# Earlier gate weights, smaller first LayerNorm groups, and a moved token mean in a macaron of routed experts, attention and a mixer

## The chip, the core and the metric

The kernel runs on one core of one Trainium2 chip. A core has a matrix engine (PE), a vector engine (DVE), a scalar engine (ACT), a general engine (POOL) that also starts the indirect DMAs, and a sync engine (SP) that issues the plain DMAs. They run their own instruction streams and meet at semaphores. The metric is the device time of one execution, in microseconds (us).

## The reference

Tokens are x, (2, 2048, 256), that is 4096 tokens of 256 numbers. Six residual steps follow one another:

```
x = x + 0.5 * ffn0(layernorm(x))          # routed to 8 experts, capacity 512 each
x = x + attn(layernorm(x))                # 16 heads, scores by a small MLP, context from sorted scores
x = x + 0.5 * ffn0(layernorm(x))
x = x + 0.5 * ffn1(layernorm(x))          # routed to 8 experts, two products, no capacity
x = x + mixer(layernorm(x))               # relu(shifted mix @ W_in), scan along tokens, @ W_out
x = x + 0.5 * ffn1(layernorm(x))

layernorm(x): (x - mean) / sqrt(var + 1e-5), over the 256 numbers of a token
routing:      logits = x @ wg (+ bg in ffn1); expert = argmax; place of a token = how many came before it at its expert
attn:         q, k = x @ Wq + bq, x @ Wk + bk ; scores = gelu(q @ W1 + b1) @ W2 + b2, the same for k
              v = x @ Wv + bv ; vc = v - mean of v over the tokens of a batch
```

## The kernel before

Tokens stand as 32 tiles of 128 tokens (`X`, called residual in the rows; `XN`, the normalised tokens, is normed). The program is a row of stages: route 0 and its experts, attention, route 1 and its experts, route 2 and its experts, the mixer, route 3 and its experts. Each engine's program is one written order of instructions; nothing is scheduled by a planner. What the order of an engine says, it does in that order, and a wait holds up everything that stands behind it on that engine.

**LayerNorm in groups.** Every route, the attention (first 16 tiles, by `LN_HALF`) and the mixer normalise tiles by the groups of `LN_ALL`: tiles 0 to 3, 4 to 11, 12 to 19, 20 to 27, 28 to 31. For a group DVE takes statistics (`dve_statistics`: L312 for each tile, L315 for each tile; in attention, route 2 and the mixer it first adds the last stage's result to each tile, L291). ACT then takes the deviation (`act_deviation`, L327), DVE the scale and shift (`dve_scale`, L333 and L334), and ACT normalises tile by tile (`act_normalise`, L339). Statistics(lo, hi) below means that of the group of those tiles. DVE issues the statistics of group g + 1 when its loop comes to the first tile of group g, and the scale of g + 1 when it comes to the last pair of g. ACT issues the deviation of g + 1 ahead of the last pair of g.

**A route.** `pe_route`, `act_route` and `dve_route` each run steps n = 0 to 19 over 16 pairs of tiles. In step n ACT normalises pair n, copies the transposed tokens of pair n - 2 out of PSUM (L417, `LAG` = 2) and the logits of pair n - 4 (L426). PE transposes pair n (L363), multiplies pair n - 3 by the gate weights `WG` (L372) and turns the logits of pair n - 4 (L384). After the last L384 of eight tiles (`GROUP` = 8) PE waits for DVE's choice and counts the tokens of each expert (L390, L392). `dve_place` (L464 to L495) is the routing of one group of eight tiles: g = 0 to 3, which I call place 0 to 3. It waits for the L384 of its fourth pair, finds the maximum (L474 in routes 2 and 3, L476), the choice (L480, for which PE waits), the position from the counts (L489), and writes the slot numbers of its eight tiles (L495). In the order of DVE, places 0 to 3 stand at the end of steps 7, 11, 15 and 19.

`pool_route` waits for the slots and for all eight normalised tiles, copies the means and deviations beside the tokens (L545, L546), and starts eight indirect DMAs, one per tile, that scatter the tokens to their slots (L548). In route 0 it waits, ahead of the first group, for the fills of the expert buffers (`emptied`, L1566). The experts' stage reads what was scattered.

**The loads.** At the start SP issues the five loads of x (L1558; tiles 0 to 3, 4 to 7, 8 to 15, 16 to 23, 24 to 31), the gate weights (L1560, two), the gate bias (L1561), two biases (L1563) and then the eight fills (L1566). In route 0 DVE waits for the gates and the constants behind the scale of tiles 0 to 3.

**Attention.** Batch 0 and batch 1 are 16 tiles each. `dve_prepare` reduces the transposed tokens of a batch to their mean (L1211, L1213), adds the biases to the projections (L1222) and, behind the eight projections of q, adds the value bias to the mean row. PE runs the 16 projections (L989), with the mean times Wv (L1001) between those of q and those of k. Then comes the hidden loop of eight steps over 512 tokens each: turn (L1015), hidden products (L1028 to L1030), scores (L1040) on PE; L1238, L1247 and L1249 on DVE. W1 is used as a high and a low part; DVE subtracts to get the low part (L1193) ahead of batch 0.

**The mixer** runs over eight chunks of four tiles. DVE issues the statistics and scales of the chunk's tiles, then two scans of the chunk before (L1516), then the input mix of this chunk (`e_mixed`, L1525). PE turns the chunk's pairs (L1415), multiplies the mixed input of the chunk before (L1427) and the states of the one before that (L1439). ACT normalises four tiles, copies the turned pairs (L1471), applies the relu (L1479) and scales the old tokens (L1489).

## Time and profile before

| what | value |
|---|---|
| time, median of 3 runs | 1492.84 us (1490.77 to 1497.94) |
| the profiled execution's own time | 1492.67 us |
| its span in the trace | 1491.2 us |
| mean granted clock of PE over the span | 0.883 of full |
| busy share: PE, DVE, ACT, POOL | 73%, 64%, 54%, 45% |
| DVE starts on route 0 / 1 / 2 / 3 at | 4.94 / 904.81 / 1039.56 / 1321.18 us |
| last scatter of route 0 / 1 / 2 / 3 starts at | 77.27 / 967.89 / 1112.57 / 1384.87 us |

The span starts with the first and ends with the last instruction of the trace; the rest of the execution's own time, 1.5 us, lies around it. A row of a timeline gives the start, the duration, the engine, the line, what is written from what, how often, and in brackets how long the engine was idle ahead of it and what released it. Rows of one shape that follow each other are one row with a count. A granted clock of 1.00 is PE at 2.4 GHz, 0.50 at 1.2 GHz.

### The profile page before, as it was taken

The page shows a single profiled execution, that of the slowest core. Times are in us where ns is not written, and L with a number is a line of the kernel's source. Part 1 is how long each engine was busy: PE and PEld are TensorE (multiplying, and loading weights), DVE is VectorE, ACT ScalarE, POOL GpSimd, SP SyncE. Part 2 cuts the span into 40 slices and gives each one's busy share as a digit, 9 for nine tenths or more (in the row PEclk, how much of TensorE's full clock was granted, in tenths as well). Part 3 has the DMA queues.
Part 4 walks back from the last instruction along what each step waited for, and adds up shares of the span by engine and source line. Part 5 has one row for each costly group of instructions (what it writes and reads, how often), then busy time and mean ns, then how long its engine had stood idle before and what let it go on. Part 6 is the DMA issues. An engine that isn't in the chain of part 4 may idle for free. (4 is left out here: it accounts for less than half of the span.)

```text
span 1491.2 us, 29986 instructions
## 1 busy us (share of the span) xinstructions
PE 1086.0 (73%) x12088; PEld 893.1 (60%) x12088; DVE 959.4 (64%) x1541; ACT 809.9 (54%) x908; POOL 665.1 (45%) x648
## 2 busy tenths in 40 slices
PE   4464689468989989909988986374639956876597
PEld 2253575368888887608888883153318943543597
DVE  4212754799999973579999995223833437764365
ACT  4311444389999933249999995222613325553232
POOL 3744000736666630073666663745162430227244
PEclk9778699779999999959999998787768987997799
DMA  9667300402112100101212112265233441003343
GB/s 286 239 205 239 93 1 0 174 30 87 69 76 87 59 8 0 34 27 59 87 59 87 69 49 95 101 217 189 73 127 96 123 156 39 1 1 111 97 123 100
DMA packets 84587, 140.59 MB, mean 94 GB/s; under 512 B 10574, under 2 KB 71246, under 8 KB 79950
## 3 DMA queue, kind: packets, MB, share of 16 engines
q1 hardware_dynamic: 71396, 102.81, 21.4%
q0 software_dynamic: 13056, 35.87, 6.7%
q8 instruction: 99, 1.62, 0.4%
q14 instruction: 36, 0.29, 0.1%
HBM read 86.62 MB, written 56.27 MB: 96 GB/s over the span
## 5 line engine op out<-in xcount | busy, mean ns | idle before, releaser
L1176 ACT ACTIVATE b_signs<-b_q_everywhere,normed 128x2048 bf16<-128x2048 f32 x224 | 430.1, 1991 | 23.9 <-PE banks L1086 20.9
L1086 PE MATMUL banks<-b_value_parts,b_signs 128*128 128x102 bf16 x8192 | 392.6, 209 | 38.6 <-DVE b_signs L1316 36.5
L1086 PEld LDWEIGHTS banks<-b_value_parts,b_signs 128*128 128x128 bf16 x8192 | 376.5, 97 | 61.8 <-DVE b_signs L1316 56.7
L1316 DVE TENSOR_SCALAR b_signs<-b_q_everywhere,normed 128x2048 bf16<-128x2048 f32 x288 | 395.9, 1434 | 2.2 <-PE banks L1086 2.0
L548 POOL DMA_INDIRECT moe_slots<-normed,slot_of_token x128 | 124.0, 969 | 39.3 <-issue 33.2
L363 PE MATMUL banks<-identity,normed 128*128 128x128 f32 x256 | 50.2, 331 | 64.5 <-ACT normed L339 48.2
L1374 POOL TENSOR_TENSOR normed<-b_sums,normed 128x16 f32<-128x16 f32 x32 | 35.0, 1095 | 135.5 <-DVE b_sums L1327 135.5
L1350 POOL TENSOR_TENSOR b_signs<-b_signs,normed 128x1024 f32<-128x1024 f32 x8 | 22.0, 2755 | 161.0 <-DVE normed L1266 160.5
L312 DVE BATCH_NORM_STATS2 ln_stats<-residual 128x6 f32<-128x256 f32 x192 | 73.8, 419 | 18.6 <-DMA bg<-in_bg 7.5
L1078 PE MATMUL banks<-normed,ones_bf 128*128 128x408 bf16 x128 | 28.9, 350 | 69.5 <-DVE normed L1284 69.5
L363 PEld LDWEIGHTS banks<-identity,normed 128*128 128x128 f32 x256 | 32.7, 164 | 72.5 <-ACT normed L339 53.4
L372 PE MATMUL banks<-normed_T,wg 128*8 128x256 f32 x256 | 73.2, 413 | 0.0
L339 ACT ACTIVATE normed<-residual,ln_shift,ln_rstd 128x256 f32<-128x256 f32 x128 | 68.6, 586 | 2.0 <-DVE ln_shift L334 2.0
L327 ACT ACTIVATE ln_std<-ln_mean_var,eps 128x4 f32<-128x4 f32 (+1 forms) x32 | 9.4, 293 | 108.2 <-DVE ln_mean_var L315 108.2
L725 POOL DMA_INDIRECT expert_rows<-d_expert_out,d_rows x40 | 38.7, 968 | 65.0 <-DVE d_expert_out L871 58.9
L725 POOL DMA_INDIRECT out_tokens<-f_expert_out,f_rows x40 | 38.4, 961 | 65.4 <-DVE f_expert_out L867 59.3
L1380 POOL TENSOR_TENSOR normed<-normed 128x256 f32<-128x256 f32 x32 | 44.6, 1393 | 41.8 <-DVE normed L1334 41.7
L1327 DVE TENSOR_REDUCE b_sums<-banks 128x544 f32<-128x1632 f32 x32 | 59.1, 1846 | 2.3 <-PE banks L1086 2.3
L1078 PEld LDWEIGHTS banks<-normed,ones_bf 128*128 128x128 bf16 x128 | 10.9, 99 | 75.7 <-DVE normed L1284 70.3
L687 DVE TENSOR_TENSOR a_expert_out<-banks,a_b 128x512 f32<-128x512 f32 x16 | 11.1, 692 | 64.3 <-PE banks L645 62.7
L1139 ACT ACTIVATE b_q_or_k_T<-banks 128x512 fp32r<-128x512 f32 x32 | 17.6, 595 | 59.1 <-PE banks L1015 59.1
L1548 POOL TENSOR_TENSOR residual<-residual,e_out_tmp 128x512 f32<-128x512 f32 x16 | 20.4, 1293 | 65.3 <-DVE e_out_tmp L1534 65.3
(253 smaller groups left out, 2474.2 us busy)
## 6 DMA issues: line engine op xcount, KB each, us to landing
b_q_everywhere<-q_rows SPq DMA_DIRECT2D x32, 1024.0 KB, 4.6
normed<-expert_rows SPq DMA_DIRECT2D x9, 1024.0 KB, 10.0
d_rows<-moe_slots SPq DMA_DIRECT2D x40, 129.5 KB, 2.1
f_rows<-moe_slots SPq DMA_DIRECT2D x40, 129.5 KB, 2.2
moe_slots<-a_empty SPq DMA_DIRECT2D x8, 518.0 KB, 8.0
a_rows<-moe_slots SPq DMA_DIRECT2D x16, 259.0 KB, 4.1
moe_empty_slots<-a_empty SPq DMA_DIRECT2D x8, 518.0 KB, 5.3
moe_slots<-moe_empty_slots SPq DMA_DIRECT2D x1, 4144.0 KB
```

The lines of the kernel that those rows point to most:

```text
L312: marks.append(k.vs.mark(nc.vector.bn_stats(k.STATS[:, t % 8, :], k.X[:, t, :])))
L339: return k.nc.scalar.activation(dst, k.X[:, t, :], ACT.Identity, bias=k.SHIFTS[:, t:t + 1], scale=k.RSTD[:, t:t + 1])
L363: ins = nc.tensor.transpose(k.bank[n % 3][:, (2 * c + i) * P:(2 * c + i + 1) * P], k.XN[:, 2 * n + i, c * P:(c + 1) * P], k.IDENT[:, :])
L372: ins = nc.tensor.matmul(k.bank[3 + p % 2][0:E, 0:2 * P], wg[:, c, :], k.XTR[:, p % 3, :, :, :].rearrange("p i k c -> p (i k c)")[:, c * 2 ...
L548: nc.gpsimd.indirect_dma_start(out=slots, out_offset=bass.IndirectOffsetOnAxis(ap=k.SLOT[:, t:t + 1], axis=0), in_=k.XN[:, t, :], in_offse ...
L725: nc.gpsimd.indirect_dma_start(out=to, out_offset=bass.IndirectOffsetOnAxis(ap=t.XS[:, n % RING_X, i, D:D + 1].bitcast(I32), axis=0), in_= ...
L1078: nc.tensor.matmul(bank[:, 0:QPB * VP].rearrange("p (i c) -> p i c", i=QPB), k.ONESB[:, :], t.HELD3[:, h, :].unsqueeze(1).broadcast_to([P, ...
L1086: ins = nc.tensor.matmul(banks[qt // QPB][:, qt % QPB * VP:(qt % QPB + 1) * VP], t.SG[:, (hh * TB + kt) % RING, qt * P:(qt + 1) * P], t.VO ...
L1176: nc.scalar.activation(t.SG[:, g % RING, :], t.QB[:, hh % 2, :], ACT.Sign, bias=t.NKT[:, kt, hh % H:hh % H + 1]).then_inc(s.sign_a, 1)
L1316: nc.vector.tensor_scalar(t.SG[:, g % RING, :], t.QB[:, hh % 2, :], t.KTM[:, kt, hh % H:hh % H + 1], 2.0, ALU.is_gt, ALU.mult).then_inc(s. ...
L1327: nc.vector.tensor_reduce(t.A[:, hh % 2, :, :].rearrange("p (b i) c -> p b i c", i=QPB), parts, AX_X, ALU.add).then_inc(s.sum, 1)
L1380: step(nc.gpsimd.tensor_tensor(t.CT, t.CT, t.N1[:, r, :].unsqueeze(2).broadcast_to([P, TB, DH]), ALU.mult))
```

## The change

Four things change.

- **Gate weights.** SP issues them and the gate bias behind the load of tiles 0 to 3, ahead of the other four loads of x. DVE's wait for them moves from behind the first scale to ahead of place 0.
- **LayerNorm groups.** The second group is split: tiles 4 to 7 and 8 to 11 are groups of their own, in all routes, attention and mixer. The deviation of group 1 is issued at tile 4, behind the normalising of tiles 0 to 3, no longer ahead of tiles 2 and 3.
- **Places.** `dve_place` stands at the top of step n = 6, 10, 14, 18, ahead of that step's statistics.
- **Attention.** The subtraction for W1's low part moves behind the 16 projections, the reduction to the mean moves in two halves into steps 2 and 3 of the hidden loop, the mean product to step 7 of it, and the row operations behind it. The mean product uses another PSUM bank.

The diff, cut (the same two edits of ACT stand again in attention and mixer; `LN_BASE` counts the semaphore values on):

```diff
@@ -47,11 +47,11 @@
...
-LN_ALL = ((0, 4), (4, 12), (12, 20), (20, 28), (28, 32))
-LN_HALF = ((0, 4), (4, 12), (12, 16))
+LN_ALL = ((0, 4), (4, 8), (8, 12), (12, 20), (20, 28), (28, 32))
+LN_HALF = ((0, 4), (4, 8), (8, 12), (12, 16))
...
@@ -404,8 +404,10 @@
...
             g = next(i for i, (lo, hi) in enumerate(LN_ALL) if lo <= t < hi)
-            if t == LN_ALL[g][1] - 2 and g + 1 < len(LN_ALL):
+            if g and t == LN_ALL[g][1] - 2 and g + 1 < len(LN_ALL):
                 act_deviation(k, n0 + g + 1, *LN_ALL[g + 1])
+            if t == LN_ALL[1][0]:
+                act_deviation(k, n0 + 1, *LN_ALL[1])
             if t == LN_ALL[g][0]:
                 nc.scalar.wait_ge(s.scale, n0 + g + 1)
             act_normalise(k, t, k.XN[:, t, 0:D]).then_inc(s.xn, 1)
...
@@ -435,10 +437,12 @@
...
-    if r == 0:
-        nc.vector.wait_ge(s.consts, 1)
-        nc.vector.wait_ge(s.gates_in, 48)
     for n in range(pairs + LAG + 2):
+        if n > LAG and 2 * (n - LAG) % GROUP == 0:
+            if r == 0 and 2 * (n - LAG) == GROUP:
+                nc.vector.wait_ge(s.consts, 1)
+                nc.vector.wait_ge(s.gates_in, 48)
+            dve_place(k, r, 2 * (n - LAG) // GROUP - 1)
         for t in (2 * n, 2 * n + 1) if n < pairs else ():
...
@@ -446,8 +450,6 @@
                     dve_statistics(k, stage, n0 + g + 1, *LN_ALL[g + 1])
                 if t == LN_ALL[g][1] - 2:
                     dve_scale(k, n0 + g + 1, *LN_ALL[g + 1])
-        if n - LAG - 1 > 0 and 2 * (n - LAG - 1) % GROUP == 0:
-            dve_place(k, r, 2 * (n - LAG - 1) // GROUP - 1)
...
@@ -975,7 +977,6 @@
...
     if batch == 0:
         nc.tensor.wait_ge(s.att_in, 16 * 8)
-        nc.tensor.wait_ge(s.w1_lo, 1)
     else:
...
     nc.tensor.wait_ge(s.at_xt, TB // 2 * (batch + 1))
@@ -993,19 +994,19 @@
...
-        if q == 0:
-            nc.tensor.wait_ge(s.mb, batch + 1)
-            if batch:
-                nc.tensor.wait_ge(s.sum, H * batch)
-            for c in range(KD):
-                ins = nc.tensor.matmul(k.bank[4][:, 0:D], t.MB[:, c, :], t.W["wv"][:, c, :], start=(c == 0), stop=(c == KD - 1))
-            ins.then_inc(s.mean, 1)
...
             if n == 0:
                 nc.tensor.wait_ge(s.hm, 16 * (batch + 1))
+                nc.tensor.wait_ge(s.w1_lo, 1)
+            if n == steps - 1:
+                nc.tensor.wait_ge(s.mb, batch + 1)
+                nc.tensor.wait_ge(s.at_xt, TB)
+                for c in range(KD):
+                    ins = nc.tensor.matmul(k.bank[5][:, 0:D], t.MB[:, c, :], t.W["wv"][:, c, :], start=(c == 0), stop=(c == KD - 1))
+                ins.then_inc(s.mean, 1)
...
@@ -1032,15 +1033,16 @@
...
         if 0 <= i < steps:
             nc.tensor.wait_ge(s.gt, hid0 + 2 * i + 2)
-            if i == 0:
-                nc.tensor.wait_ge(s.row, batch + 1)
-            else:
+            if i:
                 nc.tensor.wait_ge(s.z, 8 * batch + i)
+            elif batch:
+                nc.tensor.wait_ge(s.sum, H * batch)
...
     pe_values(k, batch, 1)
+    nc.tensor.wait_ge(s.row, batch + 1)
     for q in range(2):
...
@@ -1189,8 +1193,6 @@
...
-    nc.vector.wait_ge(s.w1_hi, 1)
-    nc.vector.tensor_tensor(t.W1R[:, 1, :, :], t.W["wp1"], t.W1R[:, 0, :, :].bitcast(F32), ALU.subtract).then_inc(s.w1_lo, 1)
     for batch in range(B):
...
@@ -1207,11 +1209,6 @@
...
 def dve_prepare(k, batch):
     nc, s, t, step = k.nc, k.s, k.at, k.vs.step
-    nc.vector.wait_ge(s.at_xt, TB // 2 * (batch + 1))
-    step(nc.vector.tensor_reduce(t.MEANS[:, :], t.XT[batch][:, :, :], AX_X, ALU.add))
-    for c in range(KD):
-        ins = nc.vector.tensor_scalar(t.MB[:, c, :], k.ONESF[:, :], t.MEANS[:, c:c + 1], 1.0 / S, ALU.mult, ALU.mult)
-    ins.then_inc(s.mb, 1)
     nc.vector.wait_ge(s.att_in, 16 * 8)
     nc.vector.wait_ge(s.bqk_in, 32 * (batch + 1))
...
@@ -1225,10 +1222,9 @@
...
             if batch == 0:
                 dve_rest(k, 8 * q + n)
-        if q == 0:
-            nc.vector.wait_ge(s.mean, batch + 1)
-            step(nc.vector.tensor_tensor(t.ROW[:, 1, :], k.bank[4][:, 0:D], t.BVB[:, :], ALU.add))
-            nc.vector.tensor_tensor(t.ROW[:, 0, :], t.BVB[:, :], t.ROW[:, 1, :], ALU.subtract).then_inc(s.row, 1)
+    if batch == 0:
+        nc.vector.wait_ge(s.w1_hi, 1)
+        nc.vector.tensor_tensor(t.W1R[:, 1, :, :], t.W["wp1"], t.W1R[:, 0, :, :].bitcast(F32), ALU.subtract).then_inc(s.w1_lo, 1)
...
@@ -1247,6 +1243,18 @@
...
             mark = k.vs.mark(nc.vector.bn_stats(t.ZST[:, q, ch, :], z))
+        if n in (2, 3):
+            if n == 2:
+                nc.vector.wait_ge(s.at_xt, TB // 2 * (batch + 1))
+            c = n - 2
+            step(nc.vector.tensor_reduce(t.MEANS[:, c:c + 1], t.XT[batch][:, c, :], AX_X, ALU.add))
+            ins = nc.vector.tensor_scalar(t.MB[:, c, :], k.ONESF[:, :], t.MEANS[:, c:c + 1], 1.0 / S, ALU.mult, ALU.mult)
+            if c == KD - 1:
+                ins.then_inc(s.mb, 1)
+        if n == steps - 1:
+            nc.vector.wait_ge(s.mean, batch + 1)
+            step(nc.vector.tensor_tensor(t.ROW[:, 1, :], k.bank[5][:, 0:D], t.BVB[:, :], ALU.add))
+            nc.vector.tensor_tensor(t.ROW[:, 0, :], t.BVB[:, :], t.ROW[:, 1, :], ALU.subtract).then_inc(s.row, 1)
...
@@ -1452,8 +1460,10 @@
         if c < NC:
...
     nc, s, a = k.nc, k.s, k.a
-    for sem, (lo, hi) in zip((s.x_in0, s.x_in1, s.x_in2, s.x_in3, s.x_in4), CUTS):
-        nc.sync.dma_start(k.X[:, lo:hi, :], tiles_of(a["x"])[:, lo:hi, :]).then_inc(sem, 16)
+    nc.sync.dma_start(k.X[:, 0:CUTS[0][1], :], tiles_of(a["x"])[:, 0:CUTS[0][1], :]).then_inc(s.x_in0, 16)
     for n in range(2):
         nc.sync.dma_start(k.WG[n][:, :, :], a[f"wg{n}"].rearrange("(k p) e -> p k e", p=P)).then_inc(s.gates_in, 16)
     nc.sync.dma_start(k.BG1[:, :], a["bg1"].partition_broadcast(P)).then_inc(s.gates_in, 16)
+    for sem, (lo, hi) in zip((s.x_in1, s.x_in2, s.x_in3, s.x_in4), CUTS[1:]):
+        nc.sync.dma_start(k.X[:, lo:hi, :], tiles_of(a["x"])[:, lo:hi, :]).then_inc(sem, 16)
     for n, name in enumerate(("b1", "b2")):
         nc.sync.dma_start(k.BIAS[:, n, :], a[name].rearrange("o (p c) -> p (o c)", p=P)).then_inc(s.biases_in, 16)
     nc.sync.wait_ge(s.empty_made, 1)
```

Where instructions stand on DVE in route 1, from the scale of tiles 12 to 19 on. 128x8 and x8 are groups of eight tiles, x4 of four. Before:

```order
L333 RECIPROCAL ln_rstd<-ln_std 128x8
L334 SCALAR_TENSOR_TENSOR ln_shift<-ln_mean_var,ln_rstd 128x8
L312 BN_STATS ln_stats<-residual 128x6 x8
L315 BN_AGGR ln_mean_var<-ln_stats 128x2 x8
L476 TENSOR_REDUCE r_max<-banks 128x8
...
L495 CAST slot_of_token<-r_slot 128x8
L333 RECIPROCAL ln_rstd<-ln_std 128x8
L334 SCALAR_TENSOR_TENSOR ln_shift<-ln_mean_var,ln_rstd 128x8
L312 BN_STATS ln_stats<-residual 128x6 x4
L315 BN_AGGR ln_mean_var<-ln_stats 128x2 x4
```

And now (lines are two further down):

```order
L333 RECIPROCAL ln_rstd<-ln_std 128x8
L334 SCALAR_TENSOR_TENSOR ln_shift<-ln_mean_var,ln_rstd 128x8
L478 TENSOR_REDUCE r_max<-banks 128x8
...
L497 CAST slot_of_token<-r_slot 128x8
L312 BN_STATS ln_stats<-residual 128x6 x8
L315 BN_AGGR ln_mean_var<-ln_stats 128x2 x8
L333 RECIPROCAL ln_rstd<-ln_std 128x8
L334 SCALAR_TENSOR_TENSOR ln_shift<-ln_mean_var,ln_rstd 128x8
L478 TENSOR_REDUCE r_max<-banks 128x8
```

Place 0 was behind statistics(20, 28) and is ahead of it; place 1 was behind statistics(28, 32) and is ahead of that. The other routes have the same order, with L291 ahead of every L312 in route 2.

On ACT at the start of the mixer, chunks 0 to 2 (e_x_T is the turned pair, e_old the scaled old tokens, e_h the relu). Before:

```order
L327 ACTIVATE ln_std<-ln_mean_var,eps 128x4
L339 ACTIVATE normed_T<-residual,ln_shift,ln_rstd 128x256 x2
L327 ACTIVATE ln_std<-ln_mean_var,eps 128x8
L339 ACTIVATE normed_T<-residual,ln_shift,ln_rstd 128x256 x2
...
L339 ACTIVATE normed_T<-residual,ln_shift,ln_rstd 128x256 x4
...
L339 ACTIVATE normed_T<-residual,ln_shift,ln_rstd 128x256 x2
L327 ACTIVATE ln_std<-ln_mean_var,eps 128x8
L339 ACTIVATE normed_T<-residual,ln_shift,ln_rstd 128x256 x2
```

And now:

```order
L327 ACTIVATE ln_std<-ln_mean_var,eps 128x4
L339 ACTIVATE normed_T<-residual,ln_shift,ln_rstd 128x256 x4
...
L327 ACTIVATE ln_std<-ln_mean_var,eps 128x4
L339 ACTIVATE normed_T<-residual,ln_shift,ln_rstd 128x256 x2
L327 ACTIVATE ln_std<-ln_mean_var,eps 128x4
L339 ACTIVATE normed_T<-residual,ln_shift,ln_rstd 128x256 x2
...
L339 ACTIVATE normed_T<-residual,ln_shift,ln_rstd 128x256 x2
L327 ACTIVATE ln_std<-ln_mean_var,eps 128x8
L339 ACTIVATE normed_T<-residual,ln_shift,ln_rstd 128x256 x2
```

Chunk 0 has one deviation less and chunk 1 two more. The deviation in chunk 2 stays where it was (tiles 12 to 19, ahead of tiles 10 and 11), but the statistics that it reads are now issued by DVE in chunk 2, no longer in chunk 1.

On PE in batch 1 of attention (batch 0 likewise), the projections before:

```order
L989 MATMUL banks<-b_wq,b_x_T 128x256 x32
L1001 MATMUL banks<-b_wv,b_means_everywhere 128x256 x2
L989 MATMUL banks<-b_wk,b_x_T 128x256 x32
L1015 MATMUL banks<-identity,b_value_parts 128x128 x16
L1028 MATMUL banks<-b_q_or_k_T,b_hidden_weights 128x512
L1029 MATMUL banks<-b_q_or_k_T,b_hidden_weights 128x512
```

And the last step of the hidden loop now:

```order
L1031 MATMUL banks<-b_q_or_k_T,b_hidden_weights 128x512
L1041 MATMUL banks<-b_signs,b_wp_110 16x512 x2
L1008 MATMUL banks<-b_wv,b_means_everywhere 128x256 x2
L1016 MATMUL banks<-identity,b_value_parts 128x128 x8
L1029 MATMUL banks<-b_q_or_k_T,b_hidden_weights 128x512
```

The mean product stands ahead of the eight turns of the last 512 tokens, behind the scores of the step before.

## Rows read from the trace of the kernel before

**Rows 1.** timeline of POOL in route 1 (start us, us, operation [idle before <-releaser])

```profile
926.83 0.20 POOL L545 COPY normed<-ln_mean_var 128x8 f32<-128x8 f32 x1 [19.93 <-DVE slot_of_token L495]
...
947.94 0.23 POOL L545 COPY normed<-ln_mean_var 128x8 f32<-128x8 f32 x1
```

**Rows 2.** timeline of DVE in route 1, around the first two place calls

```profile
923.88 0.23 DVE L476 TENSOR_REDUCE r_max<-banks 128x8 f32<-128x64 f32 x1 [2.89 <-PE banks L384]
...
932.73 0.22 DVE L476 TENSOR_REDUCE r_max<-banks 128x8 f32<-128x64 f32 x1 [4.09 <-PE banks L384]
```

**Rows 3.** line L1566 by itself, the eight fills (duration, first and last start, landing)

```profile
L1566 SPq DMA_DIRECT2D moe_slots<-a_empty x8: 382/1250/1780, 12.2 to 20.5; - x8
...
DMA to landing us min/median/max: 5.4/8.0/12.5
```

**Rows 4.** timeline of DVE in route 0

```profile
16.31 2.71 DVE L312 BATCH_NORM_STATS2 ln_stats<-residual 128x6 f32<-128x256 f32 x8 [7.53 <-DMA bg<-in_bg]
```

**Rows 5.** timeline of POOL in route 0

```profile
36.05 0.20 POOL L545 COPY normed<-ln_mean_var 128x8 f32<-128x8 f32 x1 [23.82 <-DVE slot_of_token L495]
```

**Rows 6.** timeline of PE in attention, batch 0, first projections

```profile
170.01 17.02 PE L989 MATMUL banks<-b_wq,normed 128*128 128x256 f32 x64 [2.04 <-DVE b_hidden_weights L1193]
186.86 1.03 PE L1001 MATMUL banks<-b_wv,b_means_everywhere 128*128 128x256 f32 x4
```

**Rows 7.** timeline of DVE in attention: batch 0 hidden loop, batch 1

```profile
224.27 0.74 DVE L1247 TENSOR_SCALAR b_q_everywhere<-banks,b_bp 16x512 f32<-16x512 f32 x1 [2.97 <-PE banks L1040]
...
540.52 4.36 DVE L1211 TENSOR_REDUCE b_means<-b_x_T 128x2 f32<-128x4096 f32 x1
...
546.93 2.48 DVE L1222 TENSOR_TENSOR b_value_parts<-banks,b_sums 128x512 f32<-128x512 f32 x4 [1.53 <-issue]
```

**Rows 8.** timeline of DVE in route 2, from the start of statistics(20, 28)

```profile
1060.36 0.48 DVE L291 SCALAR_TENSOR_TENSOR residual<-normed,r_gate,residual 128x256 f32<-128x256 f32 x1
...
1067.14 0.63 DVE L315 BATCH_NORM_AGGREGATE ln_mean_var<-ln_stats 128x2 f32<-128x6 f32 x8
1067.80 0.22 DVE L474 TENSOR_TENSOR logits<-banks,bg 128x64 f32<-128x64 f32 x1
...
1070.82 0.17 DVE L495 CAST slot_of_token<-r_slot 128x8 int32<-128x8 f32 x1
```

**Rows 9.** timeline of ACT in route 2

```profile
1063.29 1.08 ACT L339 ACTIVATE normed<-residual,ln_shift,ln_rstd 128x256 f32<-128x256 f32 x2
...
1065.01 1.08 ACT L339 ACTIVATE normed<-residual,ln_shift,ln_rstd 128x256 f32<-128x256 f32 x2
...
1067.80 0.30 ACT L327 ACTIVATE ln_std<-ln_mean_var,eps 128x8 f32<-128x8 f32 x1 [0.97 <-DVE ln_mean_var L315]
```

**Rows 10.** timeline of PE in route 2, logits and the turn for place 0

```profile
1065.09 1.03 PE L372 MATMUL banks<-normed_T,wg 128*8 128x256 f32 x4
1066.05 0.28 PE L384 MATMUL banks<-identity,d_logits_T 8*128 8x8 f32 x2
...
1070.76 1.88 PE L372 MATMUL banks<-normed_T,wg 128*8 128x256 f32 x4
```

**Rows 11.** timeline of POOL in route 2, third group of scatters

```profile
1092.50 0.21 POOL L545 COPY normed<-ln_mean_var 128x8 f32<-128x8 f32 x1
```

**Rows 12.** timeline of DVE in the mixer: statistics(12, 20), mix of chunk 1

```profile
1242.74 0.42 DVE L291 SCALAR_TENSOR_TENSOR residual<-normed,residual 128x256 f32<-128x256 f32 x1
...
1249.05 0.63 DVE L315 BATCH_NORM_AGGREGATE ln_mean_var<-ln_stats 128x2 f32<-128x6 f32 x8
...
1251.97 1.26 DVE L1525 SCALAR_TENSOR_TENSOR e_mixed<-e_x_T,e_scalars,e_old 128x1024 f32<-128x1024 f32 x1
```

**Rows 13.** timeline of PE in the mixer, input products of chunk 1

```profile
1253.88 5.30 PE L1427 MATMUL banks<-e_mixed,e_w_in 128*128 128x512 f32 x8
```

**Rows 14.** timeline of DVE in route 3, first place call

```profile
1340.29 0.22 DVE L474 TENSOR_TENSOR logits<-banks,bg 128x64 f32<-128x64 f32 x1 [2.89 <-PE banks L384]
```

**Rows 15.** timeline of POOL in route 3, third group of scatters

```profile
1364.86 0.20 POOL L545 COPY normed<-ln_mean_var 128x8 f32<-128x8 f32 x1
```

10 lines of the change are left out of this document (7 added, 3 removed).

## The prediction

> **What bounds the kernel now.** No engine does: PE is busy 73% of the span, POOL 45%. So I read the timelines stage by stage and asked in each which wait ends last.
>
> In the four routes it is POOL. Once the slots of eight tiles are there, POOL's groups of eight scatters follow one another without a gap: in route 1 the first group starts at 926.83 and the third at 947.94, so 10.56 us a group [rows 1]. Place 1 is there long before it is wanted: place 0 starts at 923.88 and place 1 at 932.73, 8.85 us later, with a group of scatters taking 10.56 [rows 2]. A route therefore ends at a fixed distance behind place 0, and places 1 to 3 have slack; the slack of place 1 is 10.56 - 8.85 = 1.7 us. That number is the point on which this change turns. In route 0 the first group waits for something else too: the last of the eight fills is issued at 20.5 and the slowest takes 12.5, which gives 33.0 [rows 3], while POOL starts at 36.05, released by the slots [rows 5].
>
> In attention's projections and hidden loop it is PE: in each step DVE waits 2.97 us for PE's scores [rows 7]. In the mixer's first chunks it is the chain from DVE's statistics over ACT to PE.
>
> **Route 0.** DVE waits 7.53 us for the gate bias ahead of statistics of tiles 4 to 11, which start at 16.31 [rows 4]. With the gates behind the first load of x this wait goes; next late are the other loads of x (three more issues of SP stand ahead of them), and the slots could come about 6 us earlier, an estimate: the wait of 7.5 less 1.5 for loads that land later. But POOL also waits for the fills, 33.0 by [rows 3] against 36.05 [rows 5]: the gain is 36.05 - 33.0 = **-3.0**. The fills are moved by nothing, as SP issues the same work ahead of them. Bounds: -2 (the fills land later beside other loads) to -6 (they land earlier).
>
> By the Trainium skill, "DMA: Bandwidth & Descriptors", the table at its head, transfers below 512 bytes don't reach line rate; the gate weights are rows of 32 bytes and now stand ahead of 28 of the 32 tiles of x, which would eat into the 6 us and not into the 3.0, so by this rule the sum stays.
>
> **The routes behind a moved place.** What is needed to work out places 1 and 2 is the loop that the new order closes. Statistics(20, 28) now stand behind place 0 on DVE. ACT wants their deviation ahead of normalising tiles 18 and 19, and the logits of pair 7, for which place 1 waits, are copied by ACT three pairs behind that (it copies pair n - 4 in step n). So place 1 cannot start before: place 0, plus DVE's time in it, plus statistics(20, 28), plus the way from there to place 1. The terms:
> - place 0 until DVE is free: 1070.82 + 0.08 less 1067.80 = 3.1 in routes 2 and 3 [rows 8]; 2.7 in routes 0 and 1, which have no bias row and the shorter wait for the counts (an estimate from the two fewer steps there).
> - eight tiles of statistics: 2.71 [rows 4] and the aggregation's 0.63 [rows 8], less their overlap, 3.25. With the addition, from 1060.36 to 1067.14 + 0.63, 7.4 [rows 8]. Four tiles are 1.7 and 3.8.
> - from the deviation to the next place: 0.2, by which ACT's next normalising follows the one at 1067.80 [rows 9], two pairs on ACT at 1065.01 - 1063.29 = 1.72 [rows 9], and 3.05 from the start of the third pair to its place: ACT began pair 7 at 1063.29 [rows 9], copied pair 3's logits behind it, and PE's turn of those, the last that place 0 needs, ended at 1066.05 + 0.28 [rows 10]. Together 0.2 + 3.44 + 3.05 = **6.7**.
>
> Route 1. The smaller second group lets pairs 2 and on start earlier: 4 tiles instead of 8 in the first deviation, which saves 3.25 - 1.7 = 1.6; the one group more adds a wait of which I keep 0.3: place 0 at 923.88 - 1.3 = 922.6 [rows 2]. Place 1 = 922.6 + 2.7 + 3.25 + 6.7 = 935.3, that is 12.7 behind place 0 where 10.56 is the limit. Statistics(28, 32) likewise stand ahead of place 2: 935.3 + 2.7 + 1.7 + 6.7 = 946.4. Its slots come 2.8 later, POOL's third group starts at 949.35 and not 947.94 [rows 1]: **+1.4**.
>
> Route 2, where each tile is added first, is the dear one. Before, place 0 started at 1067.80 without idle time, behind statistics(20, 28) [rows 8], though its logits were turned at 1066.05 + 0.28 [rows 10]: moving it ahead can give 1.5 at most. One more group costs 0.8 of handshake, so place 0 starts at 1067.2. Place 1 = 1067.2 + 3.1 + 7.4 + 6.7 = 1084.4 (17.2 behind). Place 2 = 1084.4 + 3.1 + 3.8 + 6.7 = 1098.0, slots 3.1 later, POOL's third group 1101.2 against 1092.50 [rows 11]: **+8.7**. ACT's deviation at 1067.80 [rows 9] moves to 1077.7. DVE's additions there now run beside POOL's scatters; for that I add nothing, and up to 0.5 in the bound.
>
> Route 3: place 0 at 1340.29 [rows 14] - 1.3 = 1339.0; place 1 = 1339.0 + 3.1 + 3.25 + 6.7 = 1352.0; place 2 = 1352.0 + 3.1 + 1.7 + 6.7 = 1363.5; POOL 3.3 later, 1366.8 against 1364.86 [rows 15]: **+1.9**.
>
> Bounds for these three: the way of 6.7 could be 6.2 (PE and ACT find nothing ahead of them) or 7.5 (PE at half clock in it, below); it enters twice a route, so +-1 to 1.5 each.
>
> **Mixer.** Statistics(12, 20) stood in chunk 1 on DVE, from 1242.74 to 1249.05 + 0.63, in the time in which PE did the products of chunk 0 [rows 12]. They are now issued at tile 8, in chunk 2, behind the mix of chunk 1, which ends at 1251.97 + 1.26 [rows 12], or some 0.5 later as chunk 0's chain has two deviations more in chunk 1. ACT needs them ahead of tiles 10 and 11, and PE turns these ahead of the products of chunk 1. So: 1253.8 + 6.9 = 1260.7; normalising and turning, 1.9; products of chunk 1 at 1262.6 against 1253.88 [rows 13]: +8.7. The start of chunk 0 gains some 3 us by the shorter first wait, but statistics(8, 12) then stand ahead of its products, and it is gone. The later chunks wait for each other as before; they take back 0.5: **+8.2**. Bounds: +3.3 if the later chunks have slack in DVE that takes it back, +12 if PE, idle for 9 us, runs the products behind at half clock.
>
> **Attention.** Batch 0: PE idled 2.04 for W1's low part [rows 6]; it now starts 1.6 earlier and pays 0.6 ahead of the hidden loop for the subtraction. The mean product, 1.03 with 0.86 to PE's next start [rows 6], cost nothing between the projections, where DVE's additions set the end, and costs its 0.9 in the loop, where PE does: -1.6 + 0.6 + 0.9 = -0.1. The halves of the reduction, 2.2 each (4.36 [rows 7] halved), fit into DVE's 2.97 wait [rows 7] and stay hidden; if not, 0.3 a step. Batch 1: the reduction goes, but the first bias addition waits 1.53 more at 546.93 anyway [rows 7], for the loads of the biases, and still does; the mean product only changes its place: 0. Sum **-0.1**, from -1 to +1.5.
>
> **PE's clock.** After an idle stretch the same four matmuls took 1.88 and not 1.03 [rows 10]. In routes 1 to 3 PE now idles some 4 us longer ahead of pair 9 and again ahead of pair 13, so a pair there takes 1.5 more before it is back. One of each falls in the way to place 1 or 2 and is on the path: **+4.5** for three routes, from 0 to 6.
>
> The Trainium skill, "TensorE: Matmul & The Clock Gate", "What's actually happening", says that the slow clock is the default and activity lifts it. [Rows 10] agrees: 1.88 against 1.03. Without any such effect the sum would be 1509.8 and with it 1514.3.
>
> **Sum.** -3.0 + 1.4 + 8.7 + 1.9 + 8.2 - 0.1 + 4.5 = +21.6, on 1492.67 of the profiled execution: **1514.3 us**. The median of the runs, 1492.84, is the same to 0.2. Own range of this case: 1506 to 1521.
>
> **Rivals.**
> - POOL's queue hides the later places. A route then ends at its fixed distance behind place 0: -3.0 - 1.3 - 0.6 - 1.3 in the four, and the mixer's earlier start makes up for its later statistics: **1486.5**. It decides at 10.56 us from place 0 to place 1. For it: the slack in [rows 1, 2]. Against: 12.7, 17.2 and 13.0 by the loop above. 0.07.
> - Smaller costs of the same sign: the clock adds nothing and the mixer 3.3. -3.0 + 1.4 + 8.7 + 1.9 + 3.3 - 0.1 = +12.2: **1504.9**. For it: route 0 has the same clock and 3 us of slack. 0.18.
> - The mixer keeps its 3 us of earlier start and the clock adds nothing: 12.2 - 3.3 - 3 = +5.9, **1498.6**, no measurable change. 0.10.
> - Half clock through the stretches behind each new wait, mixer +12, clock +6, ways of 7.5: **1524 to 1526**. 0.08.
>
> **How the numbers follow.** The forecast has 0.57. A measurement of this kernel can tell 0.5% from no change, 7.5 us. Faster: the first rival, 0.07. Same: the third, 0.10. Slower: the rest, 0.83. The range 1502 to 1524 leaves out the first and third rivals and part of the last.
>
> **What would show it.** In the trace after: in route 2, the deviation of tiles 20 to 27 near 1077 behind an idle ACT, place 1 some 17 us behind place 0, and idle time of POOL ahead of its second and third group (there was none); the same, smaller, in routes 1 and 3. In route 0 POOL's first group near 33, released by the fills. In the mixer an idle PE of 8 us ahead of the products of chunk 1. Wrong it would be if POOL's groups still follow without a gap, if the deviation of tiles 20 to 27 is not what ACT waits for, or if the mixer's chunk 1 starts its products before its chunk 2 statistics end.

## The result and the profile after

| | kernel before | changed kernel |
|---|---|---|
| median | 1494.05 us (1490.77 to 1497.94, 4 runs) | 1524.89 us (1520.72 to 1527.03, 4 runs) |
| profiled execution, span | 1492.67, 1491.2 us | 1525.55, 1524.1 us |
| granted clock of PE | 0.883 | 0.877 |

The ratio is 1.0202, 95% interval 1.0168 to 1.0236: slower, as forecast, by 30.8 us where 21.6 were forecast. 1524.89 is 0.9 us over the upper end of the forecast's range, 1502 to 1524, and 3.9 over the 1521 of the prediction's narrower "own range". The two profiled executions are 32.9 us apart (spans 1491.2 and 1524.1), and these 32.9 are what the table splits (33.0 by its rounded rows). A route is measured from ACT's first deviation in it to the start of POOL's fourth group of scatters, route 0 to the start of its last scatter; the mixer from its first deviation to that of route 3; the experts from the fourth group to the next first deviation, or to the end.

| stage | before | after | difference | forecast |
|---|---|---|---|---|
| route 0 | 77.27 | 78.24 | +1.0 | -3.0 |
| its experts, attention | 829.26 | 829.58 | +0.3 | -0.1 |
| route 1 | 51.87 | 56.68 | +4.8 | +1.4 and 1.5 of clock |
| route 2 | 59.66 | 73.62 | +14.0 | +8.7 and 1.5 |
| mixer | 93.32 | 101.50 | +8.2 | +8.2 |
| route 3 | 52.46 | 57.45 | +5.0 | +1.9 and 1.5 |
| experts 1, 2, 3 | | | -0.6, +0.9, -0.6 | 0 |

The largest, route 2, on DVE, with lines two further down than in [rows 8] where they stand behind the edit:

```profile
1074.12 0.23 DVE L476 TENSOR_TENSOR logits<-banks,bg 128x64 f32<-128x64 f32 x1 [7.40 <-PE banks L384]
...
1093.67 0.23 DVE L476 TENSOR_TENSOR logits<-banks,bg 128x64 f32<-128x64 f32 x1 [8.21 <-PE banks L384]
```

and ACT in the same stretch, which answers to the last of [rows 9]:

```profile
1084.66 0.30 ACT L327 ACTIVATE ln_std<-ln_mean_var,eps 128x8 f32<-128x8 f32 x1 [10.38 <-DVE ln_mean_var L315]
```

Place 1 starts 19.55 us behind place 0. Between them stand the place, the statistics of tiles 20 to 27 (they end at 1084.62), and ACT, which idles 10.38 us for them. POOL then has to wait for slots, at its second and third group, which it never did before [rows 1, 11]:

```profile
1077.43 0.32 POOL L547 COPY normed<-ln_mean_var 128x8 f32<-128x8 f32 x1 [30.83 <-DVE slot_of_token L497]
...
1096.91 0.38 POOL L547 COPY normed<-ln_mean_var 128x8 f32<-128x8 f32 x1 [8.59 <-DVE slot_of_token L497]
...
1111.83 0.20 POOL L547 COPY normed<-ln_mean_var 128x8 f32<-128x8 f32 x1 [3.98 <-DVE slot_of_token L497]
```

PE behind the gap, the pairs whose logits place 1 needs (compare [rows 10]; four logit products of a pair take 1.03 at the full clock and 1.88 at half):

```profile
1085.99 1.12 PE L363 MATMUL banks<-identity,normed 128*128 128x128 f32 x4 [8.13 <-ACT normed L339]
1087.04 1.88 PE L372 MATMUL banks<-normed_T,wg 128*8 128x256 f32 x4
...
1090.20 1.45 PE L372 MATMUL banks<-normed_T,wg 128*8 128x256 f32 x4
...
1092.39 1.03 PE L372 MATMUL banks<-normed_T,wg 128*8 128x256 f32 x4
```

and the granted clock there (columns: stretch, its length, busy of PE, PEld, DVE, ACT and POOL, PEclk, DMA share, GB/s):

```profile
1084.70:1090.00 5.30, 4.00 (x14) 2.09 (x14) 0.37 (x2) 4.48 (x11) 2.90 (x3) 0.50 0.28 100
```

PE idled 8.13 us, and then ran at 0.50, that is 1.2 GHz, for one pair and most of the next, not for one; from 1090.0 to 1094.0 it was granted 0.86.

In the mixer, PE's products of chunks 0 and 1 (compare [rows 13]), and ACT's deviation between them:

```profile
1265.90 4.93 PE L1435 MATMUL banks<-e_mixed,e_w_in 128*128 128x512 f32 x8
...
1283.11 4.86 PE L1435 MATMUL banks<-e_mixed,e_w_in 128*128 128x512 f32 x8
```

```profile
1280.86 0.30 ACT L327 ACTIVATE ln_std<-ln_mean_var,eps 128x8 f32<-128x8 f32 x1 [7.29 <-DVE ln_mean_var L315]
```

17.2 us from one to the other, where it was 9.4, with ACT waiting for statistics(12, 20) and PE idle for 7.91 ahead of the turn, as forecast (8).

Route 0: POOL's first group (compare [rows 5]), and the slots of place 0 on DVE. These are now written at 28.56, 7.1 us earlier than in the kernel before, and POOL starts only 8.5 us behind them:

```profile
37.03 0.20 POOL L547 COPY normed<-ln_mean_var 128x8 f32<-128x8 f32 x1 [24.80 <-DMA moe_slots<-a_empty]
```

```profile
28.56 0.17 DVE L497 CAST slot_of_token<-r_slot 128x8 int32<-128x8 f32 x1
```

The fills release POOL, as forecast, but they land at 37.0, not at 33.0.

### The profile page after: what moved, and what is told of

It is laid out like the page before. It is cut to its first block and busy times, and to the rows that moved or that the text cites. A ratio compares the mean times of both kernels' runs of the same rounds, so it can differ in the third digit from the quotient of the medians.

```text
span 1524.1 us, 30018 instructions
## 1 busy us (share of the span) xinstructions
PE 1099.6 (72%) x12088; PEld 897.6 (59%) x12088; DVE 962.3 (63%) x1555; ACT 813.2 (53%) x914; POOL 666.0 (44%) x648
## 5 line engine op out<-in xcount | busy, mean ns | idle before, releaser
L363 PE MATMUL banks<-identity,normed 128*128 128x128 f32 x256 | 53.9, 349 | 83.8 <-ACT normed L339 83.8
L312 DVE BATCH_NORM_STATS2 ln_stats<-residual 128x6 f32<-128x256 f32 x192 | 74.0, 419 | 12.1 <-DMA residual<-in_x 5.9
L372 PE MATMUL banks<-normed_T,wg 128*8 128x256 f32 x256 | 80.9, 448 | 0.0
L547 POOL COPY normed<-ln_mean_var 128x8 f32<-128x8 f32 x16 | 3.5, 220 | 119.0 <-DVE slot_of_token L497 94.1
L689 DVE TENSOR_TENSOR a_expert_out<-banks,a_b 128x512 f32<-128x512 f32 x16 | 11.1, 691 | 63.4 <-PE banks L647 61.5
```

Of the source, the lines that this page charges most:

```text
L312: marks.append(k.vs.mark(nc.vector.bn_stats(k.STATS[:, t % 8, :], k.X[:, t, :])))
L363: ins = nc.tensor.transpose(k.bank[n % 3][:, (2 * c + i) * P:(2 * c + i + 1) * P], k.XN[:, 2 * n + i, c * P:(c + 1) * P], k.IDENT[:, :])
L372: ins = nc.tensor.matmul(k.bank[3 + p % 2][0:E, 0:2 * P], wg[:, c, :], k.XTR[:, p % 3, :, :, :].rearrange("p i k c -> p (i k c)")[:, c * 2 ...
```

## The experiments

The runs went to two chips. On one the kernel before takes 1494 to 1495 us, on the other 1520 to 1521, and there the traces show idle stretches of up to 16 us in the routes that no engine or DMA of the trace ends ("issue", "remote"). Of the slower chip are the runs with the places back, the places alone, the mixer's groups back, the turns of the identity as filling, the gates behind the third load, and the last two; all others are of the faster. Ratios are against the kernel before on the same chip. The changed kernel's 1.0202 has a before of 1494.05, as on the faster chip, so where a run of the slower one is set against it, two chips are compared. Lengths of stretches are compared within a chip.

**One part undone or done alone.** Places back behind the statistics of their step, everything else as changed:

```diff
-        if n > LAG and 2 * (n - LAG) % GROUP == 0:
...
-            dve_place(k, r, 2 * (n - LAG) // GROUP - 1)
         for t in (2 * n, 2 * n + 1) if n < pairs else ():
...
+        if n - LAG - 1 > 0 and 2 * (n - LAG - 1) % GROUP == 0:
...
+            dve_place(k, r, 2 * (n - LAG - 1) // GROUP - 1)
```

> The changed kernel with the four places back behind the statistics of their step; gate weights, small groups and attention as changed. Theory (the loop through the places costs the routes their time): route 0 keeps POOL's first group at 37.0, and POOL's groups follow without a gap again in routes 1, 2 and 3, so that the stretches from POOL's first to its fourth group shrink from 35.8, 45.0 and 37.6 us to 31.5 to 32.0 each. That takes off 4.3 + 13.1 + 5.9 = 23, to 1501 to 1503 us. Rival (the idle PE at half clock is the cost, whatever the order of DVE): the gaps of ACT at tiles 18 and 26 stay in part, and less than 12 us come off, 1513 us or more.

Measured 1.0053 (1.0031 to 1.0074). Against the 1.0202 of the changed kernel that is 1.49% less, 22.3 us of 1494, where 23 were expected. The expected times in us don't apply, as it is the other chip. The gapless groups of POOL are seen in a later run with the same order of DVE on the faster chip (the fills first, below); the first and the fourth group of route 2 (the second and third, at 1085.63 and 1096.14, have no idle time ahead of them either):

```profile
1074.86 0.20 POOL L548 COPY normed<-ln_mean_var 128x8 f32<-128x8 f32 x1 [31.04 <-DVE slot_of_token L498]
...
1106.65 0.21 POOL L548 COPY normed<-ln_mean_var 128x8 f32<-128x8 f32 x1
```

31.8 us for the three intervals, where the changed kernel takes 45.0. The rival (half clock, whatever the order) falls. One pair of runs shows the same within the faster chip: the changed kernel with a wait on SP and the run with the fills first (both below) differ only in the places and the mixer's groups, 1526.85 us in one run against 1492.06. POOL's four groups of routes 1 to 3 take 120.1 us together in the one and 95.2 in the other, the mixer 102.4 and 92.0.

The new place of the four calls alone, on the kernel before:

```diff
+        if n > LAG and 2 * (n - LAG) % GROUP == 0:
+            dve_place(k, r, 2 * (n - LAG) // GROUP - 1)
         for t in (2 * n, 2 * n + 1) if n < pairs else ():
...
-        if n - LAG - 1 > 0 and 2 * (n - LAG - 1) % GROUP == 0:
-            dve_place(k, r, 2 * (n - LAG - 1) // GROUP - 1)
```

> The kernel before with nothing but the places moved ahead of their step's statistics. Theory: places 1 and 2 wait for statistics that stand behind the place before them, in all four routes: in route 2 place 1 some 19.5 us behind place 0, POOL's four groups over 31.5 to 32 us in route 0 (it has slack there), 35.8, 45.0 and 37.6 in routes 1 to 3; place 0 of route 2 starts 1.5 earlier. Together 22 us slower than before, 1514 to 1518. Rival (it costs so much only with the small groups, which bring one handshake more in front of it): under 12 us slower.

Measured 1.0174 (1.0140 to 1.0208), 26.5 us slower on that chip, more than the 22 expected. It costs this without the small groups too, and the rival falls. Where the surplus lies is not shown: in route 0 the four groups took 40.8 us where 31.5 to 32 were expected, with an idle stretch of 9.73 us ahead of place 2 that the trace ascribes to nothing of the core, but routes 1 and 3 have such a stretch too (8.32 and 9.65), and there is no trace of the kernel before from that chip.

The mixer's groups back as they were (a table of its own for the mixer with (4, 12) in one, and the deviation ahead of a group's last pair):

```diff
+LN_MIX = ((0, 4), (4, 12), (12, 20), (20, 28), (28, 32))
...
-                if g and tile == LN_ALL[g][1] - 2 and g + 1 < len(LN_ALL):
+                if tile == LN_MIX[g][1] - 2 and g + 1 < len(LN_MIX):
```

> The changed kernel with the mixer's LayerNorm groups and deviations as they were before; all else as changed. Theory: the statistics of tiles 12 to 19 run in chunk 1 again, the products of chunk 1 start 9.4 us behind those of chunk 0 and not 17.2, and the mixer is 8.2 us shorter: 1516 to 1517. Rival (the later chunks would have waited for something else all the same): the products of chunk 1 move, the mixer's end moves by less than 4: 1521 or more.

Measured 1.0155 (1.0117 to 1.0193), 7 us less than the changed kernel's ratio gives, though the two intervals overlap; the lengths in the traces carry the reading. The products of chunks 0 and 1 stand 9.5 us apart again:

```profile
1275.69 5.03 PE L1436 MATMUL banks<-e_mixed,e_w_in 128*128 128x512 f32 x8
...
1285.19 5.29 PE L1436 MATMUL banks<-e_mixed,e_w_in 128*128 128x512 f32 x8
```

and from the first deviation of the mixer to that of route 3 it is 93.4 us, against 101.7 in the run with the places back, which has the small groups in the mixer, on the same chip: 8.2 (93.44 against 101.67). The rival, less than 4, falls.

The small groups in the routes alone, on the kernel before, by a table that only the routes use:

```diff
+LN_ROUTE = ((0, 4), (4, 8), (8, 12), (12, 20), (20, 28), (28, 32))
...
-            if t == LN_ALL[g][1] - 2 and g + 1 < len(LN_ALL):
+            if g and t == LN_ROUTE[g][1] - 2 and g + 1 < len(LN_ROUTE):
...
+            if t == LN_ROUTE[1][0]:
+                act_deviation(k, n0 + 1, *LN_ROUTE[1])
```

> The kernel before with tiles 4 to 7 and 8 to 11 as groups of their own in the four routes only, the deviation of group 1 at tile 4; attention, mixer, loads and places as before. Theory (the earlier start is lost as PE's clock rises later): measured from the first statistics of a route, place 0 of routes 1 and 3 comes within 0.7 us of 19.07 and 19.1, and in route 2 0.8 later; POOL's groups follow without a gap; all in all within 2 us of before. Rival (what I forecast): place 0 of routes 1 and 3 comes 1.3 earlier.

1492.75 in one run, before 1494.8 (1491.55 to 1496.13). From the first deviation of route 1 to place 0 it took 16.66 us (before 17.35, changed kernel 17.94), in route 3 18.06 (before 17.38). So the groups move place 0 by -0.7 and +0.7, and never by the -1.3 of the forecast. What decides between these is taken up below.

Attention's moves alone, on the kernel before; the edit is the part of the change's diff in the attention functions, without `LN_HALF` and its deviations:

```diff
-    step(nc.vector.tensor_reduce(t.MEANS[:, :], t.XT[batch][:, :, :], AX_X, ALU.add))
...
+            step(nc.vector.tensor_reduce(t.MEANS[:, c:c + 1], t.XT[batch][:, c, :], AX_X, ALU.add))
```

> The kernel before with the moves inside attention only: low part of W1, mean reduction and mean product, row operations. Theory: batch 0 starts its projections 1.5 us earlier and gives it back ahead of and in the hidden loop; batch 1's projections keep waiting for the loads of the biases. From the last normalised tile of batch 0 to the start of route 1 the time is within 1 us of before. Rival (the reduction of 4.4 us a batch was on the path): 3 us or more come off.

1495.09 in one run, before 1494.8. From attention's first deviation to the last scores of batch 0's hidden loop it took 109.2 us, as before (109.1): the earlier start is given back. In batch 1 the reduction is gone, and the first bias addition waits for the bias load. The row of the changed kernel, against [rows 7]:

```profile
548.84 2.48 DVE L1219 TENSOR_TENSOR b_value_parts<-banks,b_sums 128x512 f32<-128x512 f32 x4 [7.03 <-DMA b_sums<-in_bk]
```

In [rows 7] the wait of 1.53 ahead of this addition was marked "issue"; only now does the row name the load.

From its first deviation to that of route 1 the whole stage was 4.3 us shorter in this run (753.4 against 757.7), so the expectation, within 1 us, was missed. 2.8 of it lie between the start of batch 1's projections and the last scores of its hidden loop (79.1 against 81.9), where the 32 products behind the bias addition took 7.46 us here, 8.85 before and 10.01 in the changed kernel, by PE's clock. A later run of the changed kernel's own attention code (the long fillings, below) has 79.0 there, where the changed kernel has 82.3. So that part has some 3 us of play between runs of one code. The stage as a whole has more: in the six traces of the faster chip with the changed kernel's attention code it took 753.8, 755.1, 756.3, 756.4, 758.0 and 758.0 us, with the old code, beside the 757.7, 757.2 and 758.5. The 4.3 us of this one run are hardly more than that play, and an effect of a few us can't be told from it.

**PE's clock.** The changed kernel with PE filled while it waits for pair 9 and pair 13:

```diff
         if n < pairs:
+            if (r, n) in WARM:
+                nc.tensor.wait_ge(s.xtr, at + n - 2)
+                for _ in range(WARM[r, n]):
+                    nc.tensor.matmul(k.bank[n % 3][:, :], k.IDENT[:, :], k.X[:, 0:2, :].rearrange("p i d -> p (i d)"), start=True, stop=True)
             nc.tensor.wait_ge(s.xn, r * NT + 2 * n + 2)
```

First with turns of the identity in place of the products:

```diff
+                for _ in range(WARM[r, n]):
+                    nc.tensor.transpose(k.bank[n % 3][:, 0:P], k.IDENT[:, :], k.IDENT[:, :])
```

> The changed kernel; PE turns the identity 12 to 44 times into the bank that pair 9 or pair 13 is about to use, in routes 1 to 3, while it would be idle waiting for the normalised tiles. The turns do nothing for the result. Theory (beyond the wait itself, the half clock of the pairs behind it is on the path: from the deviation to the next place 8.3, 9.0, 8.0 and 9.3 us where the full clock takes 6.7): with PE busy through the gap these ways are 6.7 to 6.9, and 1.5 + 3.6 + 2.6 = 7.7 come off, 1517 us. Rival (ACT's own copies set the way, the clock only shows): the ways stay above 8 and the time stays at 1524.

Measured 1.0235 (1.0202 to 1.0268): nothing gained, where 7.7 us were expected. In route 2 the 44 turns were done 3.2 us before pair 9 came, and its logits took 1.88 again; and on this chip the idle time without a releaser lies in the same stretches. It tells nothing either way.

Then with the products:

```diff
+WARM = {(1, 9): 8, (1, 13): 4, (2, 9): 17, (2, 13): 9, (3, 9): 7, (3, 13): 4}
```

> The changed kernel; while PE waits for the tiles of pair 9 or pair 13 in routes 1 to 3 it multiplies the identity with 512 columns of tokens, 4 to 17 times, into the bank that the pair is about to use. The results are overwritten. In the run with shorter fillings PE still idled 3.2 us ahead of pair 9 in route 2 and the next four logit matmuls took 1.88; where the filling reached to the end of the gap (pair 13) they took 1.03. Theory (the half clock behind the gap is on the path to places 1 and 2): all pairs behind both gaps take 1.03, the four ways from the deviation to the next place that took 8.3, 9.0, 8.0 and 9.3 us fall to 6.7 to 7.2, and the routes lose some 7 us. Rival (ACT sets the way): they stay above 8.

Measured 1.0308 (1.0245 to 1.0372). All pairs behind both gaps took 1.03, but I had taken a product for 0.45 us, which is half of one, and the filling overran: in route 2 pair 9 was turned 7.8 us behind the deviation and not 1.3. The ways stayed above 8 in four of the six, as the rival had it, but for another reason.

Then with fewer:

```diff
+WARM = {(1, 9): 3, (1, 13): 2, (2, 9): 8, (2, 13): 4, (3, 9): 3, (3, 13): 2}
```

> As the run with the long fillings, but each filling is shorter than the gap it stands in (2 to 8 products of 0.9 us). The long ones kept the clock up, and overran: in route 2 from the start of pair 9's turn to place 1 took 5.4 us and not 7.7 as in the changed kernel, while the turn itself came 6 us late. Theory: now the whole way from the deviation to the next place is 6.7 to 7.3 us at both places in routes 1 to 3, where the changed kernel has 8.3, 6.7 / 9.0, 8.0 / 9.3, 6.7; 5 to 7 us less than the changed kernel, 1.2 to 1.6% over the kernel before. Rival: the ways stay, or the filling costs what it gives.

Measured 1.0169 (1.0136 to 1.0203), 5 us less than the changed kernel, 0.1% above what was expected. The intervals of the two ratios overlap, so the lengths below carry the reading and not the total. Route 2, PE, the fillings (16 records are 8 products) and the logits of the pair behind them:

```profile
1080.09 8.46 PE L362 MATMUL banks<-residual,identity 128*128 128x512 f32 x16
...
1088.92 1.03 PE L377 MATMUL banks<-normed_T,wg 128*8 128x256 f32 x4
```

The next two pairs, at 1090.68 and 1092.45, took 1.03 too. From the deviation (1086.70) to place 1 (1093.73) it was 7.0 us.

The six ways from a deviation to the next place:

| way to | route 1, place 1 and 2 | route 2 | route 3 |
|---|---|---|---|
| forecast, without clock | 6.7, 6.7 | 6.7, 6.7 | 6.7, 6.7 |
| changed kernel | 8.3, 6.7 | 9.0, 8.0 | 9.3, 6.7 |
| PE filled to fit | 6.7, 6.7 | 7.0, 7.2 | 6.9, 6.7 |

That is 6.6 us off POOL's four groups in the three routes. The half clock behind the gaps is shown as the cause, with its size.

How many pairs are slow does not follow from the length of the gap alone. In the changed kernel, behind 8.13 us in route 2 it was one and most of the next; behind 4.47 one; behind 3.90 in route 1 two in part (1.53 and 1.50); behind 2.33 and 2.40 none; and behind 3.54 in route 3 nearly two:

```profile
1375.64 1.12 PE L363 MATMUL banks<-identity,normed 128*128 128x128 f32 x4 [3.54 <-ACT normed L339]
1376.68 1.88 PE L372 MATMUL banks<-normed_T,wg 128*8 128x256 f32 x4
...
1379.85 1.69 PE L372 MATMUL banks<-normed_T,wg 128*8 128x256 f32 x4
```

**Route 0.** The gates alone, on the kernel before, with DVE's wait for them ahead of place 0, which stays where it was:

```diff
+    nc.sync.dma_start(k.X[:, 0:CUTS[0][1], :], tiles_of(a["x"])[:, 0:CUTS[0][1], :]).then_inc(s.x_in0, 16)
     for n in range(2):
         nc.sync.dma_start(k.WG[n][:, :, :], a[f"wg{n}"].rearrange("(k p) e -> p k e", p=P)).then_inc(s.gates_in, 16)
```

> The kernel before with the gate weights and bias loaded behind tiles 0 to 3 and DVE's wait for them ahead of place 0; nothing else. Theory: the slots of place 0 come at 28 to 31, but the eight fills land at 36 to 38 instead of 33, since the small gate loads are all that is in flight while SP issues them and x and the fills start later behind them; POOL's first group starts then, 0 to 2 us later than 36.05. Rival (the fills are late for the small groups' sake or by chance): POOL's first group at 33 to 34.

1496.03 in one run, before 1494.8 (1491.55 to 1496.13). POOL starts at 36.65, released by the fills, with slots ready at 30.4; nothing is gained. Then, in the changed kernel, SP holds back the experts' weights until the fills have landed:

```diff
+    nc.sync.wait_ge(s.emptied, 16 * E)
     sp_moe0(k, 0)
```

> The changed kernel with the wait on SP alone (no weights of the first experts issued before the fills have landed). Theory: POOL's first group at 29 to 31, the second when the slots of place 1 come, at 42.8, not 10.9 behind the first: the loop through the places, hidden in route 0 by the late fills, now shows there, with POOL idle 1 to 3 us ahead of the second group and the fourth group at 65 to 66 instead of 68.75.

1526.85 in one run. POOL started at 35.85, not at 29 to 31, so the loads behind the fills are not what keeps them from landing by then; the loop in route 0 did not come to light either: when POOL's second group started at 46.70 the slots of place 1 (42.59) were there.

The same wait, with places and mixer groups back:

> The changed kernel with the places back behind the statistics, the mixer's groups back as before, and one wait more on SP: the weights of the first experts are not issued before the eight fills have landed. Theory (the fills land late because other loads share the queues with them, and they alone hold POOL in route 0): the fills land at 28 to 31 and POOL starts its first group then, 5 to 7 us earlier than before; the rest is as before within 2 us: 1487 to 1490 against 1494 of before, ratio 0.995 to 0.998. Rival (the loads that stand ahead of the fills set their time, not those behind): they land at 36 to 37 again, and it is at or over the time of before.

1492.06, ratio 0.9984 (0.9965 to 1.0003): not to be told from the kernel before, and over the 1487 to 1490 expected. POOL at 35.46. The rival (what stands ahead of the fills sets their time) is the nearer of the two, though the wait is worth something: the three runs with it have POOL start at 34.35 to 35.85, the seven with the same order of loads and no wait at 36.37 to 38.02. Last, the gates behind the third load of x, on the kernel before:

```diff
+    for i, (sem, (lo, hi)) in enumerate(zip((s.x_in0, s.x_in1, s.x_in2, s.x_in3, s.x_in4), CUTS)):
+        nc.sync.dma_start(k.X[:, lo:hi, :], tiles_of(a["x"])[:, lo:hi, :]).then_inc(sem, 16)
+        if i == 2:
+            for n in range(2):
+                nc.sync.dma_start(k.WG[n][:, :, :], a[f"wg{n}"].rearrange("(k p) e -> p k e", p=P)).then_inc(s.gates_in, 16)
...
```

> The kernel before with the gate loads behind the third load of x (tiles 0 to 15 issued ahead of them), DVE's wait for them ahead of place 0. Theory (the small gate loads, with one load of x in flight, leave the queues half empty between 4 and 8 us, and the fills land that much later): the queues move over 330 GB/s between 4 and 8 us, as before (365), and the fills are done at 33 to 34.5; POOL starts its first group then or with its slots at 32 to 34, 2 to 3 us before the 36.65 of the run with the gates behind the first load. Rival (fills are late with any gates ahead of x loads): POOL's first group at 36 to 37.5.

POOL's first group started at 34.67, released by the fills. What the queues moved from 4 to 8 us (last column, GB/s), in this run:

```profile
4.00:8.00 4.00, 0.00 (x0) 0.00 (x0) 1.69 (x8) 1.27 (x1) 4.00 (x9) 1.00 1.10 364
```

and in the changed kernel:

```profile
4.00:8.00 4.00, 0.00 (x0) 0.00 (x0) 1.68 (x8) 1.21 (x1) 4.00 (x9) 1.00 0.75 188
```

With the gates behind one load of x the queues move 188 to 255 GB/s in ten runs; behind three loads, and behind all five as before, 364 to 365 in seven. The prediction's way to a landing time (last issue of a fill plus the slowest landing) comes out right: in the 13 runs in which the fills release POOL, it starts 0.1 to 0.2 us behind that sum. But the sum itself differs from run to run:

| order of the loads | last issue + slowest landing | POOL's start, where the fills release it |
|---|---|---|
| as before, 5 runs | 33.0 (the row of the prediction), 33.7, 34.6, 34.8, 36.2 | 36.31 in the last |
| gates behind three loads, 2 runs | 34.5, 35.1 | 34.67, 35.23 |
| gates behind one load, 7 runs | 36.3, 36.6, 36.9, 37.0, 37.1, 37.3, 37.9 | 36.37 to 38.02 |
| the same, with SP's wait, 3 runs | 34.2, 35.4, 35.7 | 34.35 to 35.85 |

The run at 36.2 is the one with the small groups in the routes alone, whose loads stand as in the kernel before:

```profile
36.31 0.20 POOL L548 COPY normed<-ln_mean_var 128x8 f32<-128x8 f32 x1 [24.08 <-DMA moe_slots<-a_empty]
```

So of the 4 us that the forecast missed, some 2.5 are the gates' place (mean 37.0 against 34.5), and 1.5 are that 33.0 was the earliest of five runs of one order (mean 34.5).

**A version that is better.** Places and mixer groups back, fills first, and PE turning the identity 8 times behind the first statistics of routes 1 to 3 and twice ahead of pairs 1 to 3:

```diff
+EARLY = (8, 2, 2, 2)
...
+            if r and n < 4:
+                if n == 0:
+                    nc.tensor.wait_ge(s.stat, LN_BASE[f"route{r}"] + 1)
...
+                for _ in range(EARLY[n]):
+                    nc.tensor.transpose(k.bank[n % 3][:, 0:P], k.IDENT[:, :], k.IDENT[:, :])
```

> As the run with the fills first, and PE turns the identity 8 times behind the first statistics of routes 1 to 3 and twice ahead of pairs 1 to 3. Theory (place 0 gains nothing from smaller groups since PE's clock rises 14 us into the route): the clock rises 1 to 2 us earlier, place 0 of routes 1 and 3 comes 1 to 2 us earlier, 2 to 4 us in all. Rival (the twos stand in the way of the real turns at half clock): no gain or up to 2 us slower.

1490.49, ratio 0.9971 (0.9949 to 0.9992), 1.6 us under the run without the turns, where 2 to 4 were expected; the two intervals overlap. Place 0 of routes 1 and 3 comes 15.96 us behind the first deviation, against 17.89 and 18.04 in the run without the turns. With the gates behind the third load instead of the wait on SP:

> The changed kernel with places and mixer groups back, the gate loads behind the third load of x, and PE turning the identity 8, 2, 2 and 2 times at the start of routes 1 to 3. Theory: route 0 2 to 3 us shorter than before, place 0 of routes 1 and 3 16.0 us behind the first deviation where before has 17.4: 1.4 each, in all 5 to 8 us under before, ratio 0.994 to 0.997. Rival: only what the early turns give, as the next run.

Ratio 0.9958 (0.9931 to 0.9985), 6 us less than before on that chip; place 0 at 15.95 in both routes. The 2 to 3 us expected in route 0 did not come: POOL started at 35.23, in the next run, with the old loads, at 35.72. And the turns alone, on the kernel before:

> The kernel before with nothing but the early turns of the identity on PE in routes 1 to 3. Theory (small groups give 1.3 at place 0 once the clock is up; the turns give 0.5 by themselves, as the clock before rose at 11.5 us into the route): place 0 of routes 1 and 3 16.7 to 17.2 us behind the first deviation, time within 0.2% of before. Rival (the clock is all, the groups nothing): 16.0, as with small groups.

Ratio 0.9988 (0.9960 to 1.0016), and place 0 at 17.41 and 17.20 in routes 1 and 3, as before (17.35, 17.38). The turns alone give nothing at place 0, the groups alone -0.7 to +0.7, both together -1.4. But the turns did not lift the clock here: PE was granted 0.50 up to 921 us in route 1, and the first logits took 1.32 and 1.12, before 1.39 and 1.42. So what a full clock gives with the old groups was not measured. The rival (16.0, the groups nothing) is spoken against by the 1.12, which is nearly the full clock's 1.03 and still has place 0 at 17.20.

The traces of routes 1 and 3 put the two together. "Slow" is a set of four logit products that took over 1.03, ahead of place 0; one route whose records of the first set are incomplete is left out:

| groups | slow sets ahead of place 0 | place 0 behind the first deviation |
|---|---|---|
| small | none, 4 routes | 15.95 to 15.96 |
| small | one of 1.87 to 1.88, 8 routes | 16.52 to 16.66 |
| small | two, the second 1.69 or more, 10 routes | 17.65 to 18.06 |
| old | one of 1.12 to 1.44, 10 routes | 17.20 to 17.41 |
| old | two, 1.88 and 1.22, 1 route | 18.50 |

## Why the prediction was wrong

The direction was right, and so was the mechanism of the routes behind a moved place and of the mixer; in route 0 the sign was wrong. Three steps failed in size, by 3.3, 3.8 and 4.0 us, 11.1 together; attention adds 0.4 and the experts take off 0.3. That makes up all but 0.1 of the 11.3 between the 32.9 of the traces and the 21.6. The clock's price was taken from one slow pair behind one gap in the trace before, of 3.13 us, which stands just ahead of the last of [rows 10]:

```profile
1069.47 0.21 PE L390 MATMUL banks<-chosen_bf,upper_bf 128*128 128x72 bf16 x1 [3.13 <-DVE chosen_bf L480]
```

- **"PE's clock", +4.5.** The step took one pair per route at half clock. Measured are 1.6 + 0 in route 1, 2.3 + 1.3 in route 2 and 2.6 + 0 in route 3 on the ways to places 1 and 2, 7.8 together, of which filling PE gave back 6.6. In the changed kernel two pairs were slow, wholly or in part, behind the first gap of each of the three routes (3.90, 8.13 and 3.54 us). The bounds, "from 0 to 6", were too narrow at the top, and the upper end of the range with them.
- **"place 0 at 923.88 - 1.3".** In the changed kernel place 0 comes 0.6 us later in route 1, 0.85 later in route 2 (for -0.6) and only 0.85 earlier in route 3: 1.9 + 1.45 + 0.45 = 3.8 in all. In routes 1 and 3 a saving near 1.3 shows where the clock is up or nearly so (15.95 against 17.20 in the table above), and each slow set ahead of place 0 takes some of it back. The step saved the DVE time and left PE at the clock that it had in the row: in route 1 of the changed kernel PE took 1.88 for the logits at 915.38 and again at 918.23, where the kernel before had 1.39 and then 1.03. In route 2 the 1.5 us for moving place 0 ahead of the statistics did not come: with the small groups it stands 25.30 behind the first deviation with the places moved and 25.42 with the places back (24.45 in the kernel before). One group more, put at 0.8, cost about 1.0 there.
- **"36.05 - 33.0 = -3.0", and "The fills are moved by nothing, as SP issues the same work ahead of them".** The fills landed at 37.0, +1.0; the bound of -2 lay on the wrong side of nothing. Two things failed. The same work stands ahead of the fills, but in another order, and that moves them: 2.5 us by the means of the table above. And 33.0 was the landing in one run, where five runs of one order gave 33.0 to 36.2, mean 34.5. The trace has 188 GB/s from 4 to 8 us where it had 365. The prediction weighed the Trainium skill, "DMA: Bandwidth & Descriptors", the table at its head (no line rate below 512 bytes), for the loads of x alone; the measured drop agrees with it, and bears on the fills too. But the DMA engines' busy share fell as well, from 1.08 to 0.75, so the queues also stood partly empty while the small loads were issued; no run separates the two.
- **The mixer, +8.2**: measured 8.2. ACT waited 7.29 us for the statistics that had moved, as forecast. The products of chunk 1 came 8.9 later for the forecast 8.7; 1.1 of that is that those of chunk 0 were later too (16.0 us behind the first deviation, before 14.9), where the forecast had the start cancel out, and 7.8 the longer distance between the two. The later chunks took back 0.7 for the forecast 0.5. The sum is right to 0.1 in part because these small misses cancel.
- **The loop through places and statistics.** Without the clock it was right to 0.1 us: from a place to the next deviation 6.0, 4.4, 10.5, 6.9, 6.4 and 4.8 us for the forecast 5.95, 4.4, 10.5, 6.9, 6.35 and 4.8, and the way 6.7 where PE's clock was up.
- **Attention, -0.1**: +0.3 (with the first experts), within the play of that stage. The wait for the bias loads took the reduction's place.

**The rivals.** That POOL's queue hides the later places needed at most 10.56 us between places 0 and 1; the distances were 14.3, 19.6 and 15.6. The rival in which the mixer keeps its earlier start falls, as that start came 1.1 us later; and both this rival and the one of smaller costs had the clock add nothing, where it added 7.8. The last rival, 1524 to 1526, has the measured 1524.89 in its range, but by luck: its mixer of +12 was 8.2, its ways of 7.5 were 6.7 to 9.3, and route 0, which its sum leaves at -3.0, gave +1.0.

One sum is off by a little: the terms of route 1 put POOL's third group at 949.2, not 949.35, so +1.2 and not +1.4.

## What to carry over

A step that is moved ahead of the work it waits for is not early: work out which later step of another engine then waits for the work that now stands behind it, and whether that closes a loop whose turn is longer than the queue that hid it. When a change lengthens the gaps of PE, or lets its work start earlier, the work behind them may run at another clock than in the row it is priced from: take the price from several gaps, and give it a bound as wide as they differ. A landing time read from one run is one draw: here five runs of the same loads lay 3.2 us apart. And small loads that are moved ahead of large ones can be paid by what comes last in the same queues; here it was the fills.

## What the runs showed of the hardware

- In the changed kernel, behind 8.13 us of idle time PE was granted 0.50 (1.2 GHz) from 1084.7 to 1090.0, and two sets of logits were slow (1.88 and 1.45). Behind 4.47 us in the same route one was (1.88, then 1.03), behind 3.90 in route 1 two (1.53 and 1.50), behind 3.54 in route 3 two (1.88 and 1.69), behind 2.33 and 2.40 none. With PE kept busy through the gap by products whose results are thrown away, all took 1.03.
- One f32 product of 128x512 shows as two records, 0.44 us each at the full clock (34 records in 14.86 us).
- With two small weight loads and a bias load behind 0.5 MB of x, which SP issued in 1.5 us, the queues moved 188 to 255 GB/s from 4 to 8 us in ten runs, and 364 to 365 in the seven in which at least three loads of x were issued ahead of them.
- The eight fills, issued in the same order behind the same loads, had landed at 33.0 to 36.2 us in five runs, by last issue plus slowest landing.
- The same program took 1.8% longer on one chip than on another, with idle stretches that the trace ascribes to no engine or DMA of the core. What they are stays open.
